# Edge counts in one round: 16 buckets, one product for each block of edges, and a fifth of the row one-hots on ScalarE

## The chip, the cores and the metric

The kernel runs on one core of a Trainium2 chip. The metric is the device time of one execution in microseconds. The engines are TensorE (PE; its weight loads are shown as PEld), VectorE (DVE), ScalarE (ACT), GpSimd (POOL) and SyncE (SP), which issues most DMAs. Each works through its own instructions in order and waits for the others on semaphores.

## What is computed

A model of two layers over 1024 nodes with 512 features and 17408 directed edges (8192 random ones, their reverses, and a loop at each node; sorted by destination in the input). Layer 0: graph attention, then 8 experts of which each row takes two. Layer 1: a graph aggregation with a two-layer network, attention of 8 heads, then 8 experts of which each row takes one. The attention of layer 0 needs the adjacency matrix, the aggregation of layer 1 a matrix with the number of times each edge occurs:

```python
x = x + gnn0(layernorm(x), edge_index)     # adj[src, dst] = 1;  a = q @ k.T / sqrt(512)
                                           # softmax(a * adj + (1 - adj) * -1e6) @ v
x = x + experts0(layernorm(x))
x = x + gnn1(layernorm(x), src, dst)       # neigh = segment_sum(feat[src], dst); relu network; + feat
x = attention_and_experts1(x)              # 8 heads, 8 experts
```

The kernel makes one matrix CT of counts, CT[src, dst] (1024 x 1024). The mask of the attention is min(CT, 1), and CT goes to memory for layer 1. How CT is made is what the change touches.

## The kernel before, in words

**The stages at the front.** The first 307 of 1085 us are: the normalisation of x and its transposes; eight projections (query and key alternating, four each, "projected(i)" on VectorE) of 24 products of 512 columns, since every fp32 product is done in three passes of high and low halves; eight tiles of values; eight tiles of scores (two banks of 512 columns each); the counts; then the attention loop over eight tiles of 128 rows (mask, exponential, transposes, values, residual). For each projection ScalarE makes the high half from PSUM with the bias, VectorE the low half and the low half of a weight block that comes in its place.

**The edges, step 1: sort.** The edges lie on 128 partitions, 136 to each (EC). VectorE tells each edge its tile of 128 sources (in_tile, 8 x 136 wide), counts with a scan (seen_in), and two small products on TensorE give the ranks over the partitions. From them follows for each edge a place: a block of 128 lanes and a lane. Every tile starts a new block, so there are EDGE_BLOCKS = 136 + 8 = 144 blocks.

**Step 2: move.** 136 columns of edges are moved in 34 quads (QUADS). For a quad VectorE makes four pairs of lane one-hots times the edge's row and column number ("lanes", L1085), ScalarE four step functions over the blocks ("steps", L680), and TensorE multiplies them into bank 7: eight edge products of 145 columns ("move_edges", L1623). Two buffers each: quad q waits until quad q-2 has been multiplied. The order is written out by hand. On VectorE one call of lanes() follows projected(0) and the edge columns; then each of projected(1) to projected(7) is followed by two; each low half of a value tile by two; the rest come at the end. On TensorE a move stands after every second quarter (k = 1 and k = 3) of projections 2 to 7, of the value tiles and of the first score tiles. A wait of TensorE at a move holds all that is queued behind it.

**Step 3: count.** From bank 7 follow for each block the rows and columns of its 128 edges (block_rc). VectorE makes 144 row one-hots (count_rows, L1118, 128x128), computes the source tile of each block (tile_past, block_tile), adds the value bias to x (L1126), and makes column one-hots of half the columns, 128x512 (L1138), in groups of four blocks; of every eighth block ScalarE makes the column one-hot with two operations (absolute distance, then relu(1 - d), L713 and L720). A ring of eight groups lies between them and TensorE, which multiplies row and column one-hot of each block into the PSUM bank of its tile (L1697; the bank number comes from a register). Eight banks hold 8 tiles x 512 columns, so there are two rounds over all 144 blocks, one for each half of the columns. After each round ScalarE and VectorE copy the banks to CT (L647, L1143). Then SyncE sends CT out and the attention begins with no_edge (L742), mask (L1153, L1157) and softmax (L749).

## Time and profile before

| | |
|---|---|
| median of 3 runs | 1089.34 us (1089.09 to 1094.71) |
| profiled execution | 1087.22 us, its span 1085.4 us |
| busy in the span | PE 881.8, DVE 757.5, ACT 507.2, POOL 357.7 us |
| instructions | 13783 |

The span runs from the first to the last instruction of the profiled execution; the 1.8 us between it and the execution's own time lie around it. Busy shares of the whole span say little here, since the stages have different limits; the stretches of the first 307 us are what matter for this change. In the rows below, L and a number is a line of the kernel; an idle time stands in square brackets with the operation that ended it.

### The profile page before, as it was taken

What the parts mean: (1) busy time and instruction counts of PE and PEld (TensorE: products, weight loads), DVE (VectorE), ACT (ScalarE), POOL (GpSimd) and SP (SyncE); (2) the same over time, 40 slices, a digit from 0 to 9 for tenths busy, and PEclk for the clock granted to TensorE, in tenths of its full rate; (3) what the DMA queues carried; (4) which work ended last, traced back from release to release, by engine and by line L of the source; (5) the groups of instructions that cost most, each with busy time, mean ns of one, the idle gap of its engine ahead of it and who ended that gap; (6) DMA issues with size and microseconds to landing.
All of it is one profiled execution on the core that took longest, in us unless ns stands there. A gap on an engine that the chain in (4) does not pass through costs nothing.

```text
span 1085.4 us, 13783 instructions
## 1 busy us (share of the span) xinstructions
PE 881.8 (81%) x4522; PEld 674.3 (62%) x4522; DVE 757.5 (70%) x1550; ACT 507.2 (47%) x880; POOL 357.7 (33%) x236
## 2 busy tenths in 40 slices
PE   2999997888864999298898788999999987745990
PEld 2777773336743887077687676777777766534860
DVE  8878599886796443857122776778687877796638
ACT  3567517655652554132303046656565656643530
POOL 1000000000202553007321327686786666703520
PEclk9999999998995999589999889999999999966995
DMA  5010000007261444423111330010010050272432
GB/s 160 30 22 2 1 1 1 1 21 265 66 231 59 137 154 139 164 98 98 49 49 29 107 78 1 20 49 20 11 30 20 1 175 1 87 251 100 154 141 103
DMA packets 55523, 84.74 MB, mean 78 GB/s; under 512 B 8976, under 2 KB 31760, under 8 KB 54944
## 3 DMA queue, kind: packets, MB, share of 16 engines
q1 hardware_dynamic: 49376, 63.94, 18.7%
q0 software_dynamic: 6080, 19.93, 5.6%
q8 instruction: 39, 0.64, 0.2%
q14 instruction: 28, 0.23, 0.1%
HBM read 57.11 MB, written 22.54 MB: 73 GB/s over the span
## 4 chain that ended last, share of the span: by engine, by line
PE 57%; DVE 32%; ACT 4%; issue 3%; DMA 2%; POOL 1%; SPq 0%; DVEq 0%; ACTq 0%; POOLq 0%
PE PS L328 37%; DVE late_columns L1138 4%; DVE neg_max L1507 3%; PE PS L1934 3%; PE PS L1949 3%; DVE APL L976 3%; PE PS L1948 2%; PE PS L1923 2%; DVE count_rows L1118 2%; PE PS L1842 2%; PE PS L1623 2%; PE PS L1785 2%; DVE early_columns L1138 1%; DVE XN L1009 1%; DVE XN L1575 1%
## 5 line engine op out<-in xcount | busy, mean ns | idle before, releaser
L615 POOL TENSOR_SCALAR AP__201<-AP__201,rden 128x1024 f32<-128x1024 f32 x64 | 181.9, 2847 | 84.6 <-DVE rden L1512 83.9
L556 POOL TENSOR_TENSOR W1L<-W1R,W1H 128x1024 fp32r<-128x1024 f32 x8 | 18.9, 2390 | 292.0 <-DVE neg_max L1157 288.2
L647 ACT ACTIVATE APH<-PS 128x512 fp32r<-128x512 f32 x128 | 71.7, 597 | 68.7 <-PE PS L1934 44.1
L1507 DVE TENSOR_REDUCE neg_max<-PS 128x1 f32<-128x1024 f32 x64 | 78.2, 1222 | 34.8 <-PE PS L1923 34.0
L976 DVE TENSOR_TENSOR APL<-PS,APH 128x512 fp32r<-128x512 f32 x128 | 83.1, 680 | 24.8 <-ACT APH L647 24.6
L328 PE MATMUL PS<-XTH,WH 128*128 128x512 f32 x224 | 81.8, 412 | 4.5 <-DVE XTL L976 4.5
L1934 PE MATMUL PS<-ident,AP__201 128*128 128x128 f32 x512 | 70.7, 280 | 12.6 <-DVE APL L976 10.8
L328 PE MATMUL PS<-XTL,WH 128*128 128x512 f32 x224 | 78.4, 397 | 0.0
L328 PE MATMUL PS<-XTH,WL 128*128 128x512 f32 x224 | 78.1, 395 | 0.0
L1934 PEld LDWEIGHTS PS<-ident,AP__201 128*128 128x128 f32 x512 | 59.4, 143 | 28.8 <-issue 16.8
L547 POOL CAST WH<-RAW 128x512 fp32r<-128x512 f32 x30 | 23.4, 781 | 158.5 <-PE PS L328 93.5
L917 ACT ACTIVATE AP__201<-PS,neg_max 128x1024 f32<-128x1024 f32 x64 | 71.5, 1117 | 7.4 <-DVE neg_max L1507 6.7
L566 POOL DMA_INDIRECT BX<-normalised,gather_i x38 | 40.1, 1055 | 90.1 <-DVE scatter_i L1329 69.8
L1085 DVE SCALAR_TENSOR_TENSOR edge_lanes<-lanes,edge_lane,edge_vals 128x256 f16<-128x256 f16 x136 | 55.6, 480 | 8.2 <-PE PS L1623 8.2
L1949 PE MATMUL PS<-APH,AV 128*128 128x512 f32 x128 | 50.8, 397 | 11.1 <-DVE APL L976 11.1
L579 POOL DMA_INDIRECT expert_rows<-BY,scatter_i x38 | 37.4, 985 | 61.9 <-ACT BY L647 61.9
L1602 PE MATMUL PS<-ident,XN 128*128 128x128 f32 x128 | 28.3, 398 | 36.2 <-DVE XN L1009 15.7
L680 ACT ACTIVATE edge_steps<-blocks,edge_step 128x145 f16<-128x145 f16 x136 | 45.3, 408 | 20.7 <-PE PS L1623 17.1
L976 DVE TENSOR_TENSOR BHL<-PS,BHH 128x256 fp32r<-128x256 f32 x38 | 16.1, 425 | 51.2 <-ACT BHH L647 51.2
L1138 DVE TENSOR_SCALAR late_columns<-columns,block_rc 128x512 f16<-128x512 f16 x189 | 50.5, 355 | 0.0
L328 PEld LDWEIGHTS PS<-XTH,WH 128*128 128x128 f32 x224 | 42.2, 193 | 13.4 <-POOL WL L549 3.5
L1697 PE MATMUL PS<-late_columns,count_rows 128*128 128x512 f16 x189 | 46.8, 389 | 4.5 <-DVE late_columns L1138 2.5
(302 smaller groups left out, 2393.4 us busy)
## 6 DMA issues: line engine op xcount, KB each, us to landing
YT<-expert_rows SPq DMA_DIRECT2D x12, 512.0 KB, 6.8
counts<-CT SPq DMA_DIRECT2D x8, 512.0 KB, 4.9
W1R<-in_L_ffn_w SPq DMA_DIRECT2D x8, 512.0 KB, 3.9
W2R<-in_L_ffn_w SPq DMA_DIRECT2D x8, 512.0 KB, 5.6
normalised<-XN SPq DMA_DIRECT2D x2, 2048.0 KB, 8.7
CG<-counts SPq DMA_DIRECT2D x8, 512.0 KB, 3.4
RAW<-in_L_gnn_W SPq DMA_DIRECT2D x16, 256.0 KB, 2.8
W1R<-in_L_ffn_W SPq DMA_DIRECT2D x8, 512.0 KB, 8.7
```

The lines of the kernel that those rows point to most:

```text
L328: got = pe.matmul(o, lhs, r, start=first and j == 0, stop=last and j == 2)
L615: gp.tensor_scalar(AP_[:, i % 4, :], AP_[:, i % 4, :], rden[:, i % 4:i % 4 + 1], None, ALU.mult).then_inc(B["norm"], 1)
L647: act.activation(dst, src, Copy, **kw).then_inc(s, 1)
L680: got = act.activation(edge_steps[:, q % 2, j, 0:STEPS_OF], blocks16[:, :], ACT.Sign, bias=edge_step[:, 4 * q + j:4 * q + j + 1])
L917: act.activation(AP_[:, i % 4, :], banks(2 * (i % 2)), ACT.Exp, bias=neg_max[:, i % 4:i % 4 + 1], accum_out=denom[:, i % 4:i % 4 + 1]).the ...
L976: v.tensor_tensor(dst, src, f(hi), ALU.subtract).then_inc(s, 1)
L1085: got = v.scalar_tensor_tensor(out=edge_lanes[:, q % 2, j, :, :], in0=lanes1[:, :].unsqueeze(1).to_broadcast([P, 2, P]), scalar=edge_lane[ ...
L1138: got = v.tensor_scalar(count_columns(k, j), columns16[:, r * HALF:(r + 1) * HALF], block_rc[:, 1, b:b + 1], None, ALU.is_equal)
L1507: v.tensor_reduce(out=neg_max[:, i % 4:i % 4 + 1], in_=banks(2 * (i % 2)), axis=X_AXIS, op=ALU.max, negate=True).then_inc(B["mx"], 1)
L1697: got = pe.matmul(PS[:, ds(held[b % 24]), :].rearrange("p a n -> p (a n)"), count_rows[:, b, :], moving, start=False, stop=False, skip_gro ...
L1934: got = pe.transpose(PS[:, 4 + half, k * P:(k + 1) * P], AP_[:, i % 4, c * P:(c + 1) * P], ident[:, :])
L1949: got = pe.matmul(PS[:, 6, :], AV[:, hp % 2, h, k, :], APH[:, k, :], start=k == 0, stop=k == NT - 1)
```

## The change

Edges are sorted into 16 buckets: tile of 128 sources times half of the columns. A block then belongs to one half only, so that one product with a column one-hot of 512 columns does for each block, in one round over 136 + 16 = 152 blocks. The arrays of the sort are 16 x 136 wide instead of 8 x 136. Sixteen buckets share eight PSUM banks: bucket k lies in bank k % 8, and ScalarE copies a finished bucket to CT and, for the first eight, writes zeros into the bank. A bucket is finished when its last group has been multiplied; SyncE reads the number of that group from a table into a register and waits for it. Before each pair of groups TensorE waits for a grant from GpSimd, which reads from a table how many banks must be free. The number of the bucket of each block comes from a product on TensorE (past16). All column one-hots are made by VectorE; of the rows every fifth is made by ScalarE from the third score tile on, six behind each copy of the scores. The ring has six groups. The pieces of the sort are spread among projected(0) to projected(3), the first call of lanes() stands behind projected(3), two follow each of projected(4) to projected(7), and TensorE moves its first quad in projection 4; in the score tiles a move stands after every quarter. The value bias is added tile by tile in the attention loop, and ScalarE executes one small exponential before the last bucket. In the diff the names before16, ones16, lanes1, ident are constants; runs of removed lines and of unchanged ones are cut.

```diff
     BLOCKS = tuple((k * N + NEXP * (P - 1)) // P for k in CHOICES)
     QUADS = EC // 4
-    EDGE_BLOCKS = EC + NT
+    BUCKETS = 2 * NT
+    EDGE_BLOCKS = EC + BUCKETS
     COUNT_GROUPS = EDGE_BLOCKS // 4
     STEPS_OF = EDGE_BLOCKS + 1
-    RING = 8
...
+    RING = 6
+    SORTS = (7, 18, 29)
+    PLACED = SORTS[2] + 6
+    assert EC % 4 == 0 and COUNT_GROUPS % 2 == 0 and HB == 2 and GB == 8 and NT == 8 and KT == 4
...
                                  y_d[c * N + 2 * g * P:c * N + (2 * g + 2) * P, :].rearrange("(t p) d -> p t d", p=P)).then_inc(M["y_in"][g], 16)
-        wait(columns_used, 2 * COUNT_GROUPS)
+        wait(sort_dve, PLACED)
+        for k in range(BUCKETS - 1):
+            last = sp.value_load(last_group[0:1, k:k + 1], min_val=1, max_val=COUNT_GROUPS)
+            wait(columns_used, last)
...
                     out=y_d[:, :], out_offset=bass.IndirectOffsetOnAxis(ap=scatter_i[:, b:b + 1], axis=0),
                     in_=BY[:, g % 2, :], in_offset=None).then_inc(M["rows_out"][g % 2], 16)
+        wait(sort_dve, PLACED)
+        for g in range(COUNT_GROUPS // 2):
+            needed = gp.value_load(banks_needed[0:1, g:g + 1], min_val=1, max_val=BUCKETS)
+            wait(bank_free, needed)
+            gp.sem_inc(banks_granted, 1)
         wait(A["m2"], NT)
         expert_lo(0)
...
             act.activation(dst[:, n, :], banks(2 * (i % 2)), Identity, bias=bias[:, n:n + 1]).then_inc(Q0["hi"], 1)
             act.wait_ge(raw_in[j], 16 * (i // 4) + 32)
             copy(WH[:, i, :], RAW[:, j, :], w_hi)
-            if i:
+            if i >= 4:
                 steps()
-            steps()
+            if i >= 3:
+                steps()
         for t in range(NT):
...
             steps()
+        def row_by_act(i):
+            act.wait_ge(distanced, i + 1)
+            act.activation(count_rows[:, 5 * i + 4, :], distance[:, i % 2, :], ACT.Relu, bias=1.0, scale=-1.0).then_inc(act_rows, 1)
         for t in range(NT):
+            for _ in range(min(4, QUADS - stepped[0])):
+                steps()
             act.wait_ge(Q0["s_ps"], t + 1)
             copy(SR[:, t, :], banks((4, 0)[t % 2]), Q0["s_done"], scale=-D ** -0.5)
-            for _ in range(min(2, QUADS - stepped[0])):
...
+            if t == 2:
+                act.wait_ge(sort_dve, PLACED + 3)
+            if 2 <= t < NT - 1:
+                for i in range(6 * (t - 2), 6 * (t - 1)):
+                    if i >= 2:
+                        act.wait_ge(act_rows, i - 1)
+                    act.activation(distance[:, i % 2, :], lanes1[:, :], ACT.Abs, bias=minus_row[:, i:i + 1]).then_inc(distanced, 1)
+                    if i > 6 * (t - 2):
+                        row_by_act(i - 1)
+                row_by_act(6 * (t - 1) - 1)
         assert stepped[0] == QUADS
-        per_round = COUNT_GROUPS // 2
...
+        def count_out(k):
+            if k < BUCKETS - 1:
+                act.wait_ge(bucket_done, k + 1)
+            else:
+                act.wait_ge(columns_used, COUNT_GROUPS)
+            copy(CT[:, k // 2, k % 2 * HALF:(k % 2 + 1) * HALF], PS[:, k % 8, :], counted)
+            if k < 8:
+                act.wait_ge(counted, k + 1)
+                copy(PS[:, k, :], PS[:, k, :], bank_free, scale=0.0)
         def no_edge(half, par):
             t = 2 * half + par
-            act.wait_ge((counted_act, counted_dve)[par], NT // 2 + half + 1)
+            act.wait_ge(counted, 2 * t + 2)
             if t >= 2:
                 act.wait_ge(A["m2"], t - 1)
             act.activation(PEN[:, par, :], CT[:, t, :], ACT.Relu, bias=neg_col[:, 0:1], scale=-NEG).then_inc(A["penalty"], 1)
...
             act.wait_ge(M["w_in"][e // 4], which * (160, 96)[e // 4] + 64)
             copy(W1H[which][:, e, :, :], W1R[:, e, :, :], M["w_hi"])
-        no_edge(0, 0)
...
+        for k in range(BUCKETS):
+            count_out(k)
+            if k in (1, 3):
+                no_edge(0, k // 2)
+            if k == BUCKETS - 2:
...
         v.wait_ge(edges_in, 32)
         v.wait_ge(setup, 12)
-        per_tile = [P, NT, EC]
+        per_bucket = [P, BUCKETS, EC]
         sort(v.tensor_scalar(tile_of[:, :], src_i[:, :], 7, None, ALU.logical_shift_right))
+        sort(v.tensor_scalar(place_i[:, :], dst_i[:, :], 9, None, ALU.logical_shift_right))
         sort(v.tensor_copy(tile_f[:, :], tile_of[:, :]))
-        sort(v.tensor_tensor(in_tile[:, :, :], tile_f[:, :].unsqueeze(1).to_broadcast(per_tile),
...
+        sort(v.scalar_tensor_tensor(out=place_f[:, :], in0=tile_f[:, :], scalar=2.0, in1=place_i[:, :], op0=ALU.mult, op1=ALU.add))
+        sort(v.tensor_tensor(in_bucket[:, :, :], place_f[:, :].unsqueeze(1).to_broadcast(per_bucket),
+                             blocks16[:, 0:BUCKETS].unsqueeze(2).to_broadcast(per_bucket), ALU.is_equal))
         for t in range(NT):
...
             lo(WL[:, u, :], RAW[:, u, :], WH[:, u, :], w_ready)
         transposed(0)
-        v.wait_ge(sort_ps, 1)
...
+        in_flat = in_bucket[:, :, :].rearrange("p t c -> p (t c)")
+        sort(v.tensor_tensor_scan(seen_in[:, 1:1 + BUCKETS * EC], in_flat, in_flat, 0.0, ALU.add, ALU.max))
+        seen_before = seen_in[:, 0:BUCKETS * EC].rearrange("p (t c) -> p t c", t=BUCKETS)
+        seen = seen_in[:, 1:1 + BUCKETS * EC].rearrange("p (t c) -> p t c", t=BUCKETS)
+        sort(v.tensor_tensor(bucket_count16[:, :], seen[:, :, EC - 1], seen_before[:, :, 0], ALU.subtract))
+        assert sorts[0] == SORTS[0]
+        def bucket_bases():
+            v.wait_ge(sort_ps, 1)
+            rank, total = PS[:, 6, 0:BUCKETS], PS[:, 6, BUCKETS:2 * BUCKETS]
+            sort(v.tensor_scalar(bucket_i[:, :], total, P - 1.0, None, ALU.add))
+            sort(v.tensor_scalar(bucket_i[:, :], bucket_i[:, :], 7, None, ALU.logical_shift_right))
+            sort(v.tensor_scalar(bucket_blocks[:, :], bucket_i[:, :], 1.0, None, ALU.max))
+            sort(v.tensor_tensor_scan(bucket_end[:, :], ones16[:, 0:BUCKETS], bucket_blocks[:, :], 0.0, ALU.mult, ALU.add))
+            sort(v.tensor_tensor(bucket_base[:, :], bucket_end[:, :], bucket_blocks[:, :], ALU.subtract))
+            sort(v.scalar_tensor_tensor(out=bucket_base[:, :], in0=bucket_base[:, :], scalar=float(P), in1=rank, op0=ALU.mult, op1=ALU.add))
+            sort(v.tensor_tensor(bucket_base[:, :], bucket_base[:, :], seen_before[:, :, 0], ALU.subtract))
+            sort(v.tensor_tensor(seen, seen, bucket_base[:, :].unsqueeze(2).to_broadcast(per_bucket), ALU.add))
+            sort(v.tensor_tensor(end_mask[0:BUCKETS, :], bucket_end[0:BUCKETS, :], ident[0:BUCKETS, 0:BUCKETS], ALU.mult))
+            sort(v.tensor_reduce(out=end_col[0:BUCKETS, :], in_=end_mask[0:BUCKETS, :], axis=X_AXIS, op=ALU.add))
+            sort(v.tensor_scalar(past16[0:BUCKETS, :], blocks16[0:BUCKETS, 0:EDGE_BLOCKS], end_col[0:BUCKETS, :], None, ALU.is_ge))
+            assert sorts[0] == SORTS[1], sorts
+        def places():
+            sort(v.tensor_tensor(in_bucket[:, :, :], in_bucket[:, :, :], seen, ALU.mult))
+            sort(v.tensor_reduce(out=place_f[:, :], in_=in_bucket[:, :, :].rearrange("p t c -> p c t"), axis=X_AXIS, op=ALU.add))
+        def edge_columns():
+            sort(v.tensor_scalar(place_i[:, :], place_f[:, :], -1.0, None, ALU.add))
+            sort(v.tensor_scalar(place_i[:, :], place_i[:, :], 7, None, ALU.logical_shift_right))
+            sort(v.tensor_copy(edge_block[:, :], place_i[:, :]))
+            sort(v.scalar_tensor_tensor(out=edge_lane[:, :], in0=edge_block[:, :], scalar=-float(P), in1=place_f[:, :], op0=ALU.mult, op1=ALU.add))
+            sort(v.tensor_scalar(edge_vals[:, :, 0], src_i[:, :], 1.0, 0.5, ALU.add, ALU.mult))
+            sort(v.scalar_tensor_tensor(out=edge_vals[:, :, 0], in0=tile_f[:, :], scalar=-0.5 * P, in1=edge_vals[:, :, 0], op0=ALU.mult, op1=ALU.add))
+            sort(v.tensor_scalar(dst_i[:, :], dst_i[:, :], HALF - 1, None, ALU.bitwise_and))
+            sort(v.tensor_scalar(edge_vals[:, :, 1], dst_i[:, :], 0.5, None, ALU.mult))
+            sort(v.tensor_scalar(edge_step[:, :], edge_block[:, :], -1.0, -0.5, ALU.mult, ALU.add))
+            assert sorts[0] == SORTS[2], sorts
+        def banks_of_blocks():
+            v.wait_ge(sort_ps, 2)
+            sort(v.tensor_scalar(block_f[:, :], PS[:, 6, 2 * BUCKETS:2 * BUCKETS + EDGE_BLOCKS], BUCKETS - 1.0, None, ALU.min))
+            sort(v.tensor_copy(block_bank[:, :], block_f[:, :]))
+            sort(v.tensor_scalar(block_bank[:, :], block_bank[:, :], 7, None, ALU.bitwise_and))
+            sort(v.tensor_scalar(banks_needed[:, :], block_f[:, :].rearrange("p (g j) -> p g j", j=8)[:, :, 7], 1.0, None, ALU.add))
+            sort(v.tensor_scalar(last_group[:, :], bucket_end[:, :], 3.0, None, ALU.add))
+            sort(v.tensor_scalar(last_group[:, :], last_group[:, :], 2, None, ALU.logical_shift_right))
+            assert sorts[0] == PLACED, sorts
         def projected(i):
...
             got.then_inc(edges_laned, 1)
         projected(0)
-        sort(v.tensor_scalar(place_i[:, :], place_f[:, :], -1.0, None, ALU.add))
...
+        bucket_bases()
+        projected(1)
+        places()
+        projected(2)
+        edge_columns()
+        projected(3)
         lanes()
-        for i in range(1, 2 * KT):
+        for i in range(4, 2 * KT):
             projected(i)
+            if i == 5:
+                banks_of_blocks()
             lanes()
             lanes()
         for t in range(NT):
...
         v.wait_ge(edges_moved, QUADS)
         sort(v.tensor_copy(block_sum[:, :, :], PS[:, 7, 0:2 * STEPS_OF].rearrange("p (v b) -> p v b", v=2)))
         sort(v.tensor_tensor(block_rc[:, :, :], block_sum[:, :, 1:STEPS_OF], block_sum[:, :, 0:EDGE_BLOCKS], ALU.subtract))
-        sort(v.tensor_scalar(minus_column[:, :], block_rc[:, 1, :], -1.0, None, ALU.mult))
+        sort(v.tensor_scalar(minus_row[:, :], block_rc[:, 0, 0:EDGE_BLOCKS - 2].rearrange("p (i j) -> p i j", j=5)[:, :, 4], -1.0, None, ALU.mult))
         v.wait_ge(Q0["v_ps"], NT)
         for b in range(EDGE_BLOCKS):
+            if b % 5 == 4:
+                continue
             got = v.tensor_scalar(count_rows[:, b, :], lanes1[:, :], block_rc[:, 0, b:b + 1], None, ALU.is_equal)
         got.then_inc(rows_ready, 1)
-        per_block = [P, EDGE_BLOCKS, NT]
...
+        for k in range(COUNT_GROUPS):
+            if k >= RING:
+                v.wait_ge(columns_used, k - RING + 1)
+            elif k == 2:
+                v.wait_ge(Q0["s_ps"], NT)
+            for j in range(4):
+                b = 4 * k + j
+                got = v.tensor_scalar(count_columns(k, j), columns16[:, 0:HALF], block_rc[:, 1, b:b + 1], None, ALU.is_equal)
+            got.then_inc(columns_ready, 1)
         v.wait_ge(row0_in, 16)
-        v.tensor_tensor(X[:, :, :], X[:, :, :], row0[:, :].unsqueeze(1).to_broadcast([P, NT, D]), ALU.add).then_inc(Q0["bias"], 1)
...
+        def value_bias(t):
+            v.tensor_tensor(X[:, t, :], X[:, t, :], row0[:, :], ALU.add).then_inc(Q0["bias"], 1)
         def mask(half, par):
             t = 2 * half + par
-            v.wait_ge((counted_act, counted_dve)[par], NT // 2 + half + 1)
+            v.wait_ge(counted, 2 * t + 2)
             v.wait_ge(Q0["s_done"], NT)
             if t >= 2:
                 v.wait_ge(A["exp"], t - 1)
...
         mask(0, 0)
         mask(0, 1)
+        value_bias(0)
         p_lo(0, 0)
         for i in range(NT // 2 - 1):
             mask(i + 1, 0)
+            value_bias(2 * i + 1)
             p_lo(i, 1)
             residual(i, 0)
             mask(i + 1, 1)
+            value_bias(2 * i + 2)
             p_lo(i + 1, 0)
             residual(i, 1)
+        value_bias(NT - 1)
         p_lo(NT // 2 - 1, 1)
         v.wait_ge(gw_hi, 1)
...
             return [PS[:, b, :], PS[:, b + 1, :]]
         pe.wait_ge(setup, 12)
-        pe.wait_ge(sort_dve, SORTS[0])
...
         moved = [0]
...
                                  k == 0, k == KT - 1)
                 if k == KT - 1:
                     got.then_inc(Q0["ps"], 1)
-                if i >= 2 and k % 2:
+                if i >= 4 and k % 2:
                     move_edges()
+            if i == 0:
+                pe.wait_ge(sort_dve, SORTS[0])
+                pe.matmul(PS[:, 6, 0:BUCKETS], before16[:, :], bucket_count16[:, :], start=True, stop=True)
+                pe.matmul(PS[:, 6, BUCKETS:2 * BUCKETS], ones16[:, :], bucket_count16[:, :], start=True, stop=True).then_inc(sort_ps, 1)
+            elif i == 3:
+                pe.wait_ge(sort_dve, SORTS[1])
+                pe.matmul(PS[:, 6, 2 * BUCKETS:2 * BUCKETS + EDGE_BLOCKS], ones16[0:BUCKETS, :], past16[0:BUCKETS, :],
+                          start=True, stop=True).then_inc(sort_ps, 1)
         pe.wait_ge(w_ready, 12)
         for par in range(2):
...
                                  k == 0, k == KT - 1)
                 if k == KT - 1:
                     got.then_inc(Q0["s_ps"], 1)
-                if k % 2 and moved[0] < QUADS:
+                if moved[0] < QUADS:
                     move_edges()
         tiles = [pe.alloc_register(f"tile{j}") for j in range(24)]
         pe.wait_ge(rows_ready, 1)
-        pe.wait_ge(sort_dve, SORTS[1] + 6)
+        pe.wait_ge(act_rows, EDGE_BLOCKS // 5)
+        pe.wait_ge(sort_dve, PLACED)
         pe.wait_ge(Q0["v_done"], NT)
-        for r in range(2):
...
+        pe.wait_ge(Q0["s_done"], NT)
+        for t in range(8):
+            pe.matmul(PS[:, t, :], count_rows[:, EDGE_BLOCKS - 1, :], columns16[:, 0:HALF], start=True, stop=True).then_inc(bank_free, 1)
+        for g in range(COUNT_GROUPS):
+            if g % 6 == 0:
+                n = min(24, EDGE_BLOCKS - 4 * g)
+                pe.load(tiles[0:n], block_bank[0:1, 4 * g:4 * g + n])
+                held = [pe.snap(q, min_val=0, max_val=7) for q in tiles[0:n]]
+            if g % 2 == 0:
+                pe.wait_ge(banks_granted, g // 2 + 1)
+            pe.wait_ge(columns_ready, g + 1)
+            for j in range(4):
+                b = 4 * g + j
+                got = pe.matmul(PS[:, ds(held[b % 24]), :].rearrange("p a n -> p (a n)"), count_rows[:, b, :],
+                                count_columns(g, j), start=False, stop=False, skip_group_check=True)
+            got.then_inc(columns_used, 1)
         for q in tiles:
             pe.free_register(q)
```

## Rows read from the trace of the kernel before

**Rows 1.** The table of stretches: busy time of each engine, then granted clock, DMA share, GB/s.
```profile
27.70:81.50 53.80, 51.21 (x289) 40.81 (x289) 43.50 (x87) 30.80 (x72) 0.00 (x0) 1.00 0.13 26
81.50:114.50 33.00, 33.00 (x225) 25.47 (x226) 30.04 (x71) 24.23 (x68) 0.00 (x0) 0.95 0.01 1
114.50:134.70 20.20, 20.20 (x123) 16.02 (x122) 9.13 (x23) 9.18 (x24) 0.00 (x0) 1.00 0.00 1
134.70:162.00 27.30, 27.23 (x120) 22.15 (x119) 27.16 (x149) 4.62 (x6) 0.00 (x0) 1.00 0.00 1
162.00:248.20 86.20, 69.67 (x304) 29.97 (x305) 80.27 (x268) 57.36 (x86) 0.00 (x0) 0.96 0.07 26
```

**Rows 2.** The chain of waits, 134 to 260 us: start, duration, what.
```profile
135.93 23.53 DVE count_rows L1118 x144
...
162.42 4.44 DVE X L1126
166.88 1.93 DVE early_columns L1138 x7
168.81 5.51 DVE late_columns L1138 x21
...
241.38 2.06 ACT CT L647 x4
...
245.53 1.28 ACT L749
246.82 1.25 ACT PR L749 x2
248.21 1.95 PE PS L1710 x8
...
259.92 1.24 DVE SM L1153
```

**Rows 3.** The chain of waits, 60 to 100 us.
```profile
78.40 1.12 ACT KH L688
79.55 1.28 DVE KL L979
...
81.49 2.93 PE PS L328 x6
84.41 0.75 PE PS L1623 x8
...
90.52 0.53 PE PS L1623 x8
91.05 1.44 PE PS L328 x6
```

**Rows 4.** VectorE in order of time: start, duration, operation, idle before it.
```profile
87.87 3.25 DVE L1085 SCALAR_TENSOR_TENSOR edge_lanes<-lanes,edge_lane,edge_vals 128x256 f16<-128x256 f16 x8
91.19 0.69 DVE L976 TENSOR_TENSOR VL<-PS,VH 128x512 fp32r<-128x512 f32 x1
```

**Rows 5.** ScalarE in order of time, values and scores.
```profile
86.63 0.60 ACT L647 ACTIVATE VH<-PS 128x512 fp32r<-128x512 f32 x1
...
161.96 1.02 ACT L647 ACTIVATE SR<-PS 128x1024 f32<-128x1024 f32 x1 [4.41 <-PE PS L328]
```

**Rows 6.** VectorE in order of time, the sort of the edges.
```profile
5.67 2.43 DVE L1036 TENSOR_TENSOR_SCAN seen_in<-in_tile 128x1088 f32<-128x1088 f32 x1
...
28.98 1.29 DVE L1062 TENSOR_TENSOR seen_in<-seen_in,tile_base 128x1088 f32<-128x1088 f32 x1
...
31.64 2.25 DVE L1064 TENSOR_REDUCE place_f<-in_tile 128x136 f32<-128x1088 f32 x1
```

**Rows 7.** TensorE in order of time, behind two idle stretches.
```profile
81.49 0.79 PE L328 MATMUL PS<-WH,XTH 128*128 128x512 f32 x1 [2.59 <-DVE WL L976]
...
207.91 3.16 PE L1697 MATMUL PS<-late_columns,count_rows 128*128 128x512 f16 x7 [2.02 <-DVE late_columns L1138]
```

**Rows 8.** VectorE in order of time, in the attention loop.
```profile
264.63 1.23 DVE L976 TENSOR_TENSOR PTL<-PS,PTH 128x1024 fp32r<-128x1024 f32 x1 [2.15 <-ACT PTH L647]
```

More of the change, by code:

```diff
@@ L429, in _ @@
         results(0)
-        wait(Q0["bias"], 1)
+        wait(Q0["bias"], NT)
         sp.dma_start(row0[:, :], a["L1_gnn_b2"].partition_broadcast(P)).then_inc(row0_in, 16)
@@ L722, in counts_out @@
-        def counts_out(r):
-            act.wait_ge(columns_used, COUNT_GROUPS * (r + 1))
-            for t in range(0, NT, 2):
-                copy(CT[:, t, r * HALF:(r + 1) * HALF], PS[:, t, :], counted_act)
-        act.wait_ge(sort_dve, SORTS[1] + 3)
-        column_distance(0)
-        for i in range(2 * per_round):
-            if i + 1 < 2 * per_round:
-                column_distance(i + 1)
-            column(i)
-            if i == per_round + 1:
-                counts_out(0)
-        counts_out(1)
+            if t == 2:
+                act.wait_ge(sort_dve, PLACED + 3)
@@ L1051, in _ @@
         transposed(0)
-        v.wait_ge(sort_ps, 1)
-        tile_rank, tile_total = PS[:, 6, 0:NT], PS[:, 6, NT:2 * NT]
-        sort(v.tensor_scalar(tile_i[:, :], tile_total, P - 1.0, None, ALU.add))
-        sort(v.tensor_scalar(tile_i[:, :], tile_i[:, :], 7, None, ALU.logical_shift_right))
-        sort(v.tensor_copy(tile_blocks[:, :], tile_i[:, :]))
-        sort(v.tensor_tensor_scan(tile_end[:, :], ones16[:, 0:NT], tile_blocks[:, :], 0.0, ALU.mult, ALU.add))
-        sort(v.tensor_tensor(tile_base[:, :], tile_end[:, :], tile_blocks[:, :], ALU.subtract))
@@ L1060, in _ @@
-        sort(v.scalar_tensor_tensor(out=tile_base[:, :], in0=tile_base[:, :], scalar=float(P), in1=tile_rank, op0=ALU.mult, op1=ALU.add))
-        sort(v.tensor_tensor(tile_base[:, :], tile_base[:, :], seen_before[:, :, 0], ALU.subtract))
-        sort(v.tensor_tensor(seen, seen, tile_base[:, :].unsqueeze(2).to_broadcast(per_tile), ALU.add))
-        sort(v.tensor_tensor(in_tile[:, :, :], in_tile[:, :, :], seen, ALU.mult))
-        sort(v.tensor_reduce(out=place_f[:, :], in_=in_tile[:, :, :].rearrange("p t c -> p c t"), axis=X_AXIS, op=ALU.add))
+        in_flat = in_bucket[:, :, :].rearrange("p t c -> p (t c)")
@@ L1119, in _ @@
         got.then_inc(rows_ready, 1)
-        per_block = [P, EDGE_BLOCKS, NT]
-        sort(v.tensor_tensor(tile_past[:, :, :], tile_end[:, :].unsqueeze(1).to_broadcast(per_block),
-                             blocks16[:, 0:EDGE_BLOCKS].unsqueeze(2).to_broadcast(per_block), ALU.is_le))
-        sort(v.tensor_reduce(out=block_f[:, :], in_=tile_past[:, :, :], axis=X_AXIS, op=ALU.add))
-        sort(v.tensor_scalar(block_tile[:, :], block_f[:, :], NT - 1.0, None, ALU.min))
-        v.wait_ge(row0_in, 16)
@@ L1172, in residual @@
             v.wait_ge(A["rden"], t + 1)
+            v.wait_ge(Q0["bias"], t + 1)
             x = X[:, ds(t), :].rearrange("p a n -> p (a n)")
@@ L1673, in _ @@
         pe.wait_ge(rows_ready, 1)
-        pe.wait_ge(sort_dve, SORTS[1] + 6)
+        pe.wait_ge(act_rows, EDGE_BLOCKS // 5)
+        pe.wait_ge(sort_dve, PLACED)
         pe.wait_ge(Q0["v_done"], NT)
-        for r in range(2):
-            for t in range(NT):
-                if r:
-                    pe.wait_ge((counted_act, counted_dve)[t % 2], t // 2 + 1)
-                elif t == 0:
-                    pe.wait_ge(Q0["s_done"], NT)
-                pe.matmul(PS[:, t, :], count_rows[:, EDGE_BLOCKS - 1, :], columns16[:, 0:HALF], start=True, stop=True)
-            for g in range(COUNT_GROUPS):
-                if g % 6 == 0:
-                    pe.load(tiles, block_tile[0:1, 4 * g:4 * g + 24])
-                    held = [pe.snap(q, min_val=0, max_val=NT - 1) for q in tiles]
-                pe.wait_ge(columns_ready, COUNT_GROUPS * r + g + 1)
-                for j in range(4):
-                    b = 4 * g + j
-                    k = COUNT_GROUPS * r + g
-                    moving = count_columns(k, j)
-                    if b % 8 == 7:
-                        pe.wait_ge(act_columned, k // 2 + 1)
-                        moving = act_columns[:, k // 2 % 4, :]
-                    got = pe.matmul(PS[:, ds(held[b % 24]), :].rearrange("p a n -> p (a n)"), count_rows[:, b, :],
-                                    moving, start=False, stop=False,
-                                    skip_group_check=True)
-                got.then_inc(columns_used, 1)
@@ L1721, in values @@
             got.then_inc(A["av_ps"], 1)
-        pe.wait_ge(counted_act, NT)
-        pe.wait_ge(counted_dve, NT)
+        pe.wait_ge(counted, BUCKETS)
         p_transposes(0, 0)
```

91 lines of the change are left out of this document (25 added, 66 removed).

## The prediction

> **What bounds the kernel now.** I read the stretches of the two stages first, then the chain of waits through them, then single instructions of VectorE and ScalarE. From 27.7 to 162.0 us TensorE is busy 131.6 of 134.3 us: projections, values and scores of the first attention fill it, and the 34 quads of edge products lie between them [rows 1]. VectorE is nearly full beside it (30.0 of 33.0 us while the values are made). After 162.0 the roles change: TensorE is busy 69.7 of 86.2 us, VectorE 80.3 [rows 1]. The chain there is VectorE's one-hots: 144 rows of counts in 23.5 us from 135.9, the 4.4 us addition of the value bias, then columns without a break, 21 in 5.51 us, 0.263 each [rows 2]. It makes 126 in each of two rounds. When the last product is done, at 241.4, come copies and penalties to 245.5, a table load of 1.3 us and an exponential of 1.25 before the first probability tile is transposed at 248.2 [rows 2]. Nothing behind that tile depends on the change, save the bias.
>
> So two sums are needed: when the scores end (last copy of scores begins at 161.96 [rows 5]), and how long from there to the first transpose (248.21 − 161.96 = 86.3 us).
>
> **Part 1: after the scores, 43.8 us less.** Both rounds become one: 152 columns where 252 were made by VectorE. Rows and the first 8 columns fit under the scores as before: from the edges' end, 1.2 us of differences, 122 rows at 0.163 = 19.9, 8 columns 2.1, together 23, while TensorE has 30 us of scores left (22 quarter tiles at 5.44/4, the period of a tile being 4.41 + 1.03 [rows 5]). The shorter row list itself thus gives nothing: scores cover it, and the value bias and the table of tiles, 5 us beyond the scores' end today (166.88 against 161.96), leave the path. From the scores' end remain 144 columns × 0.263 = 37.8 us; about 0.7 for the ring of six, as TensorE starts only 3 to 4 us later (copy of scores, eight clearing products); two steps of the first mask at 1.24, 2.5 us behind the last column (they run under the final copies today); the exponential and its hand-off 1.35 [rows 2]. Sum 42.35; with a little for more hand-offs 42.5. The table load is done ahead and the copies go bucket by bucket beside the products. TensorE needs 0.96 us at most for four products (six take 1.44 [rows 3]) against VectorE's 1.05, so it isn't the bound. ScalarE copies out and clears in two half copies of 0.60, as the values' high half [rows 5], for 2.5 us of columns in a bucket. The grants of banks and the marks of finished buckets pass through register loads on GpSimd and SyncE that no row shows; I take nothing, as a pair of groups leaves them 2.1 us and eight banks lie between use and reuse. The other end is 3 us a pair, 19 × 0.9 = 17 us. ScalarE's 30 rows are two operations each, six rows in each of five tiles: at 0.60, the copy four times as wide, 7.2 us of a tile's 5.4, which would add up to 9 us; I take 0.35 for 128 elements, 4.2 us, hidden. The value bias, now eight additions of some 0.6 us, falls into VectorE's waits of 2.15 us before each low half [rows 8]; uncovered it would be 4.9 us. 86.3 − 42.5 = 43.8 us gained.
>
> **Part 2: before the scores end, what the new order of the edges costs.** I counted for each move of a quad (8 edge products) which instruction on VectorE makes its lanes. Today VectorE has laned 2i − 1 quads when it comes to "projected(i)", and TensorE, in the last quarter of projection i, wants quad 2i − 2: one in hand. In the new order there are 2i − 7 in hand (first quad after projected(3)), and TensorE (first move in i = 4) wants 2i − 6: one short. That quad is made behind projected(i), which itself waits for projection i's last product. TensorE's queue stands at the move, with the whole next projection behind it. The same holds for the values: 9 + 2t laned before tile t's low half, and its second move wants 10 + 2t. ScalarE's steps are short in the same way but come earlier. Today's margin is seen in the rows: TensorE runs through the values without a gap [rows 1], and VectorE's quads and low halves follow each other in a period of 3.32 + 0.6 = 3.92 us [rows 4].
>
> Each stall is a chain of known pieces. In a projection: ScalarE's biased copy 1.12, the low half 1.28, and the weights' low half with the hand-offs for the rest of the 3.09 us from 78.40 to 81.49 [rows 3], then one quad 1.66 [rows 4]: 4.8 us, four times, 19.2. At i = 5 six small operations for the banks come between, 1.4. At i = 7 the present wait of TensorE for the value weights (2.59 us of idle [rows 7]) is swallowed, −2.6. Together 18.0. In a value tile: high half 0.60 [rows 5], low half 0.69 and a quad 1.66 (two in the 3.32 us from 87.87 to 91.19 [rows 4]), hand-offs 0.1: 3.05 us, eight times, 24.4.
>
> The start of this: the arrays of the sort are twice as long. The scan (2.43 at 1088 elements [rows 6]) takes about 4.7, now after the last transposed tile; the addition 1.29 becomes 2.45, the product likewise, the reduction 2.25 becomes 4.45 [rows 6]. VectorE: scan and count to 31.8; projected(0) to 35.9; bases 4.5, to 40.5; projected(1) 42.4; places 6.9, 49.4; projected(2) 51.3; nine edge columns 53.8; projected(3) 55.7; first quad 57.4. TensorE comes to projection 4 at 50 and waits 1.0 us for the low half, reaches the first move at 53.4 and waits 4.0. Together 5.0.
>
> Small terms: normalisation starts earlier, since the scan leaves its front, −0.7; three small products +0.5; edge products of 153 columns for 145, 34 × 0.53 × 8/145 = +1.0 [rows 3]. Moves end in tile 2 of the scores as before, and there VectorE (1.66) keeps up with 1.36 + 0.56 us.
>
> Without the clock: 5.0 + 18.0 + 24.4 + 0.8 = 48.2 us.
>
> **The clock.** After the 2.59 us of idle before 81.49 six products take 2.93 us, not 1.44, and the eight edge products 0.75, not 0.53: the 1.2 GHz level for about 3.4 us, 1.7 us lost [rows 3, 7]. After the idle of 2.02 before 207.91 seven products take 3.16 us, where 7 × 0.24 = 1.7 would be the full rate, again the lower level [rows 7]. The new order has 13 idle stretches of 3 to 6 us. If every one costs 1.7 it is 22 us; if none does, 0, and the 1.7 paid today comes back. Some of a slow stretch passes while TensorE still idles, and a slow stretch doesn't follow every gap at once, so I take 0.6: 13.3 − 1.7 = 11.6 us. The scores end 59.8 us later.
>
> The Trainium skill ("TensorE: Matmul & The Clock Gate", HAM oscillation — how this bites in real kernels) says that a loop with waits between bursts of matmuls starts every burst at half clock and pays each time. By it the loss is the full 22, and the sum 8.7 us more. Both gaps above agree with it; thirteen in a row no row here shows.
>
> **Sum.** 59.8 − 43.8 = +16.0. The profiled execution took 1087.2 us (span 1085.4 and 1.8 around it), so 1103.2; the median of the runs is 2.1 higher, by that 1105.3. I say 1104.
>
> **Rivals.** (a) *TensorE isn't held by the short quads* (the change does what it says: half the columns). For it: 43.8 us lie on VectorE's chain and are really gone. Against it: engines work in order and the count of quads is one short in every step. It needs only the start 5.0 and 0.8: 1087.2 + 5.8 − 43.8 = 1049. The turning point is the mean cost of one of the twelve later stalls, clock included: (43.8 − 5.8)/12 = 3.2 us. Above it the change loses, below it wins; I have (18.0 + 24.4 + 11.6)/12 = 4.5. (b) *The stalls come, the clock holds*: 48.2 − 1.7 − 43.8 = +2.7, 1090 to 1092. For it: two gaps are all that I have, and the value tiles' 3.05 us lie between bursts of full work. Against: 2.02 and 2.59 us were enough. (c) *The clock falls at every gap*: 48.2 + 22 − 1.7 − 43.8 = +24.7, 1112 to 1114. (d) *Register loads on GpSimd or SyncE pace the counting*, 3 us for a pair of groups: +16 + 17, 1120 to 1122. For it: each grant and mark passes an engine that has no part in the counting today.
>
> **Chances.** Forecast with its neighbour (c): 0.72; (b) 0.10; (a) 0.11; (d) 0.07. The range takes in (b) and (c): 1090 to 1115. Within 0.5% (5.4 us) is what a measurement can't tell from no change: faster by more 0.11, within 0.11, slower by more 0.78.
>
> **What would show it.** TensorE idle in front of the edge products (the second move of each projection from 4 on and of each value tile), some 4.8 and 3.05 us each, released by VectorE's lanes; in the value tiles a period of 7 to 8.7 us, not 3.92, and a granted clock of 0.75 to 0.9; the last score copy near 222, not 162; from there to the first transpose about 42.5 us; 152 column one-hots with hardly a wait; no added idle in the attention loop. I'd be wrong if TensorE ran through the values without gaps, or if the counting took over 50 us.

## The result and the profile after

The changed kernel takes 1117.64 us (median of four, 1115.39 to 1120.88) where the kernel before takes 1090.2 (four, 1089.09 to 1094.71): ratio 1.0254, 95% interval 1.0212 to 1.0296. The forecast, 1104 with a range of 1090 to 1115, had the sign and the place of the loss right, and the part of the clock much too small. The profiled execution has a span of 1117.6 us, 32.2 more than before.

The table of stretches of the profile after has the columns of [rows 1]. The second and third stretch are the projections from the first move on and the value tiles; the fourth is the scores, the fifth goes from their end to the first transpose of the attention.

```profile
27.60:59.30 31.70, 27.12 (x111) 21.47 (x112) 26.80 (x36) 7.90 (x12) 0.00 (x0) 0.99 0.11 28
59.30:118.30 59.00, 38.55 (x168) 29.89 (x168) 21.51 (x46) 16.59 (x41) 0.00 (x0) 0.77 0.06 9
118.30:190.00 71.70, 47.83 (x233) 36.46 (x234) 34.12 (x81) 27.46 (x81) 0.00 (x0) 0.76 0.00 1
190.00:235.90 45.90, 45.84 (x244) 36.73 (x243) 34.90 (x162) 33.43 (x96) 0.00 (x0) 1.00 0.00 1
235.90:278.00 42.10, 35.72 (x160) 15.54 (x160) 41.38 (x148) 19.78 (x30) 0.00 (x0) 1.00 0.03 10
```

Where TensorE ran through [rows 1] it now idles 20.5 of 59.0 and 23.9 of 71.7 us, and the granted clock, 0.95 to 1.00 before, is 0.77 and 0.76. The list of waits of TensorE, up to 350 us (total, times, longest), names the place:

```profile
PE PS L1666 <- DVE edge_lanes L1136: 47.8, 13, 6.2
...
PE PS L335 <- DVE QL L996: 1.1, 1, 1.1
...
PE PS L1741 <- DVE early_columns L1180: 0.9, 1, 0.9
PE PS L1741 <- POOLq L520: 0.8, 1, 0.8
PE PS L1741 <- DVE late_columns L1180: 0.7, 2, 0.3
```

Thirteen waits before the edge products (L1666) for the lanes of VectorE, where the kernel before had none worth a row. The chain of waits shows two of them whole, one in projection 5, one in the first value tile (start, duration, what):

```profile
77.33 1.12 ACT KH L706
78.47 1.28 DVE KL L996
79.76 0.60 DVE WL L993
81.79 1.69 DVE edge_lanes L1136 x4
83.52 1.21 PE PS L1666 x8
84.73 5.02 PE PS L335 x12
...
118.25 0.60 ACT VH L665
118.88 0.69 DVE VL L993
119.57 1.59 DVE edge_lanes L1136 x4
121.21 1.21 PE PS L1666 x8
122.42 2.65 PE PS L335 x6
125.06 1.05 PE PS L1666 x8
```

TensorE's last product of projection 5 ends at 77.3, its next edge products begin at 83.52: copy, low half, weights, the six small operations (80.4 to 81.8), the quad. There the eight edge products take 1.21 us, not 0.56, and the twelve products behind them 5.02 us, not 2.82: the 1.2 GHz level, and not for 3.4 us as in [rows 3] but for about 5.6 us (an estimate: 1.21, and 4.4 of the 5.02, since twelve products wholly at half rate would take 5.64). The edge products come at 121.21, 130.99, 139.40, 148.12, 156.51, 165.22, 175.17 and 183.67 in the eight value tiles, a period of 8.9 us against 3.92 [rows 4].

Behind the scores all is as it was summed. First the chain of waits, then the engines in order of time at the first transpose:

```profile
235.87 1.03 ACT SR L665
237.04 1.69 PE PS L1730 x7
239.78 1.05 PE PS L1741 x4
240.85 2.19 DVE early_columns L1180 x8
243.04 4.20 DVE late_columns L1180 x16
...
272.45 2.10 DVE early_columns L1180 x8
274.55 1.14 DVE SM L1194
```

```profile
278.37 1.07 PE L1753 MATMUL PS<-ident,PR 128*128 128x128 f32 x8 [2.09 <-ACT PR L762]
...
279.28 0.69 DVE L1185 TENSOR_TENSOR X<-X,row 128x512 f32<-128x512 f32 x1
```

From the last score copy (235.87) to the first transpose (278.37) it is 42.5 us, where it was 86.3 [rows 2, 5]. One grant of GpSimd was waited for, 0.8 us.

### The profile page after: what moved, and what is told of

It reads as the page before. It is cut to its first block, busy times and chain, and to the rows that moved or that the text cites. A ratio compares the mean times of both kernels' runs of the same rounds, so it can differ in the third digit from the quotient of the medians.

```text
span 1117.6 us, 13358 instructions
## 1 busy us (share of the span) xinstructions
PE 878.6 (79%) x4379; PEld 680.3 (61%) x4379; DVE 731.3 (65%) x1436; ACT 486.0 (43%) x885; POOL 358.1 (32%) x236
## 4 chain that ended last, share of the span: by engine, by line
PE 57%; DVE 32%; ACT 4%; issue 4%; DMA 1%; POOL 1%; DVEq 0%; SPq 0%; POOLq 0%; ACTq 0%
PE PS L335 37%; PE PS L1976 3%; PE PS L1991 3%; DVE neg_max L1553 3%; PE PS L1666 3%; PE PS L1965 3%; DVE APL L993 2%; PE PS L1990 2%; PE PS L1884 2%; DVE late_columns L1180 2%; DVE edge_lanes L1136 2%; PE PS L1827 2%; DVE XN L1026 1%; DVE stats L1001 1%; DVE early_columns L1180 1%
## 5 line engine op out<-in xcount | busy, mean ns | idle before, releaser
L665 ACT ACTIVATE APH<-PS 128x512 fp32r<-128x512 f32 x128 | 71.7, 597 | 70.1 <-PE PS L1976 45.7
L1976 PE MATMUL PS<-ident,AP__204 128*128 128x128 f32 x512 | 71.2, 281 | 11.6 <-DVE APL L993 10.8
L1666 PE MATMUL PS<-edge_steps,edge_lanes 128*128 128x153 f16 x272 | 32.3, 278 | 47.8 <-DVE edge_lanes L1136 47.8
L1666 PEld LDWEIGHTS PS<-edge_steps,edge_lanes 128*128 128x128 f16 x272 | 23.9, 119 | 60.6 <-DVE edge_lanes L1136 53.6
L1648 PEld LDWEIGHTS PS<-ident,XN 128*128 128x128 f32 x128 | 23.9, 213 | 49.4 <-issue 24.2
L335 PEld LDWEIGHTS PS<-XTL,WH 128*128 128x128 f32 x224 | 44.3, 198 | 9.2
```

Of the source, the lines that this page charges most:

```text
L335: got = pe.matmul(o, lhs, r, start=first and j == 0, stop=last and j == 2)
L665: act.activation(dst, src, Copy, **kw).then_inc(s, 1)
L1648: got = pe.transpose(PS[:, t % 4, k * P:(k + 1) * P], src[:, t, k * P:(k + 1) * P], ident[:, :])
L1666: got = pe.matmul(PS[:, 7, n * STEPS_OF:(n + 1) * STEPS_OF], edge_lanes[:, q % 2, j, n, :], edge_steps[:, q % 2, j, 0:STEPS_OF], start=c = ...
L1976: got = pe.transpose(PS[:, 4 + half, k * P:(k + 1) * P], AP_[:, i % 4, c * P:(c + 1) * P], ident[:, :])
```

## The experiments

They ran in three sets, with the kernel before beside them in each (1088.9, 1089.0 and 1088.0 us). Times are medians, ratios those to the kernel before with their 95% interval. The first set is again, skip1, fill and one_ahead, the second b_short, rows_dve, fill6 and warm, the third fill2 and fillv.

**again.** The changed kernel, unchanged.

> The changed kernel once more, beside the others. Both theories: about 1117 us, ratio 1.02 to 1.03, as the granted clock of each run falls a little otherwise. It is the measure for the runs beside it.

1113.89 us, ratio 1.0236 (1.0215 to 1.0258). The last score copy begins at 228.2 us here, at 235.9 in the first profile, with the same 47.7 us of waits. TensorE is busy 152.2 us between the first projection and that copy, and was busy 159.3 us in the first profile, for the same products; 0.5 us is an earlier start. Of the 7.1 us of busy time 1.8 lie in projection 0, ahead of all the waits: in the first profile its first eight products take 3.6 us, here 1.9, though the clock row shows 1.00 for them there (fill's are as slow at the same place, with a clock row of 0.50). Projections 4 to 7 are alike in the two (38.55 and 38.60 us). The rest, 5.5 us, lies in the value tiles, where two of the eight gaps are followed by full rate here (chain of waits, the first of them):

```profile
119.02 0.71 PE PS L1666 x8
119.73 1.43 PE PS L335 x6
```

**one_ahead.** The old margin in the new kernel.

```diff
-                if i >= 4 and k % 2:
+                if i >= 5 and k % 2:
                     move_edges()
...
             projected(i)
-            if i == 5:
-                banks_of_blocks()
-            lanes()
-            lanes()
+            for _ in range((1, 3, 2, 2)[i - 4]):
+                lanes()
...
-            if i >= 4:
-                steps()
-            if i >= 3:
+            for _ in range((0, 0, 0, 1, 1, 3, 2, 2)[i]):
                 steps()
...
         while laned[0] < QUADS:
             lanes()
+        banks_of_blocks()
```

> The changed kernel with the old margin: moves start in projection 5; one quad of lanes and steps behind projections 3 and 4, three behind 5, two behind 6 and 7; the six small operations for the banks behind the last quad. My theory: no wait of TensorE over 1 us from projection 4 to the scores' end, clock 1.00, the scores end at 165 to 168 us, from there 42.5 us to the first transpose as in the changed kernel; 1087.2 + 4 - 43.9 = 1047 us (1044 to 1052). Rival (order doesn't matter): near 1117. If only part of the waits goes: 1060 to 1090.

1049.81 us, ratio 0.9638 (0.9621 to 0.9656): it is faster than both kernels. Its waits of TensorE and its stretches:

```profile
PE PS L335 <- DVE WL L991: 2.6, 1, 2.6
PE PS L335 <- DVE XTL L991: 1.4, 1, 1.4
PE PS L1663 <- DVE edge_lanes L1134: 1.4, 1, 1.4
```

```profile
27.00:80.00 53.00, 50.17 (x243) 39.90 (x243) 42.11 (x67) 21.24 (x43) 0.00 (x0) 1.00 0.13 27
80.00:165.00 85.00, 82.60 (x504) 65.28 (x505) 75.47 (x257) 64.76 (x181) 0.00 (x0) 0.98 0.00 1
165.00:210.00 45.00, 38.16 (x173) 17.30 (x172) 42.08 (x149) 21.22 (x36) 0.00 (x0) 1.00 0.04 15
```

One wait of 1.4 us instead of thirteen of 47.8 (a little over the 1.0 that was expected), the clock near 1.00, the last score copy at 167.1, the first transpose at 209.7: 42.6 us apart again. The order of the quads is the loss, and the single round is worth what was summed. (The six small operations also moved, behind the last quad; that was 1.4 us of the forecast's sum.)

**skip1.** Only TensorE's side of it.

```diff
-                if i >= 4 and k % 2:
+                if 4 * i + k > 17 and k % 2:
                     move_edges()
```

> The changed kernel, but TensorE starts its moves one place later (in the last quarter of projection 4, not in its second), so that every later move wants a quad that is one earlier. My theory (quads one short): the 4.8 us waits before the edge products of projections 4 to 7 vanish; in the value tiles the wanted quad is the second one behind the previous low half, ready 0.60 + 0.69 + 3.3 = 4.6 us after the tile before against a period of 4.0, so about 0.6 us of wait is left in each, without a fall of the clock. The scores end near 172 us instead of 236, the whole takes 1050 to 1058 us. Rival (the longer arrays of the sort and the wider edge products slow this stretch, the order doesn't matter): within 5 us of the changed kernel.

1067.25 us, ratio 0.9796 (0.9776 to 0.9817): faster than before, as the theory has it against its rival, but 9 us past the expected range. My count was wrong. The chain of waits shows which move stalls:

```profile
92.68 1.45 PE PS L335 x6
94.12 0.02 issue
94.14 0.61 ACT VH L665
94.75 0.02 issue
94.77 0.69 DVE VL L993
95.47 1.59 DVE edge_lanes L1136 x4
97.06 0.04 issue
97.10 0.71 PE PS L1666 x8
97.82 1.45 PE PS L335 x6
```

It is the first move of each value tile, not the second: it wants the first quad behind the previous low half, 3.0 us after that tile, and TensorE is there after 0.56 + 1.44 = 2.0. So TensorE waits 1.0 us in each of eight tiles, in a period of 5.14 us, and the clock stays up through the tiles. The projections aren't free of waits either, as had been expected: four waits make up the rest of 13.5 us in twelve. The longest, 2.9 us before 72.73 in projection 5, is followed by eight edge products in 1.21 us and twelve products in 5.11, so the clock fell there and cost about 2.8 us. With 13.5 us of waits where 8 × 0.6 = 4.8 were expected that is 11.5 us more than I had, against a time 9 to 17 us above the expected 1058 to 1050.

**b_short.** The reverse: the kernel before, its moves put too early.

```diff
-                if i >= 2 and k % 2:
+                if i >= 1 and k % 2:
                     move_edges()
```

> The kernel before with one condition changed: TensorE's moves start in projection 1, not in 2, so that each wants a quad two later than now (VectorE and ScalarE unchanged). Nothing of the buckets is in it. My theory (the place of the moves against the quads is the whole loss): 4.3 us before the first move, 4.8 us in each of projections 1 to 7 less the 2.6 us wait of today, 3.05 in each value tile: 59.7 us of waits, and about 2.0 us of clock for each of 16 gaps as the changed kernel showed, less 1.7: 30 us. The counting starts earlier under the scores, -7. Sum +83: 1172 us (1160 to 1182). Rival (the waits belong to the 16 buckets, their longer sort and their 153 columns): within 10 us of the kernel before.

1176.41 us, ratio 1.0797 (1.0766 to 1.0828). The waits of TensorE:

```profile
PE PS L1623 <- DVE edge_lanes L1085: 61.3, 16, 4.7
PE PS L1623 <- ACT edge_steps L680: 4.9, 2, 2.4
```

With no bucket in it, this kernel loses 87 us by one digit (each move wants a quad two later than before; 1172 was expected). So neither the longer sort nor the 153 columns are needed for the stalls.

**fill.** The stalls stay, TensorE works through them.

```diff
+        def keep_busy(n):
+            for _ in range(n):
+                pe.matmul(PS[:, 5, :], XTH[:, 0, 0:P], XTH[:, 0, 0:HALF], start=True, stop=True)
...
                 if i >= 4 and k % 2:
+                    if k == 3 or i == 4:
+                        keep_busy(19 if k == 3 else 15)
                     move_edges()
...
+                if k == KT - 1:
+                    keep_busy(12)
                 if k % 2:
                     move_edges()
```

> The changed kernel with idle products into an unused bank before each stalled move (15 before the first, 19 in each projection from 4 on, 12 in each value tile, 0.227 us each); the moves come no earlier. My theory (waits of 48 us and, apart from them, 26 us more loss by the clock than before): TensorE stays at full clock, the waits stay in length but are filled, 1117 - 24 = about 1093 us (1089 to 1097). Rival (products are slower there for another reason, or the idle time is the whole loss): no gain, 1115 us or more.

1094.4 us, ratio 1.0048 (1.0030 to 1.0066). The stretches:

```profile
60.00:110.00 50.00, 46.59 (x247) 36.88 (x246) 24.01 (x52) 19.67 (x49) 0.00 (x0) 1.00 0.04 2
110.00:167.00 57.00, 55.16 (x333) 42.95 (x332) 33.70 (x81) 26.31 (x77) 0.00 (x0) 1.00 0.00 1
```

The clock is 1.00 in both. The last score copy begins at 210.4 us, 48.4 after that of the kernel before; the sum "without the clock" was 48.2. To compare them, 1.8 has to be taken off the 48.4 for slow products in projection 0 (clock 0.50 from 26.4 to 30.1 us), and the 1.7 added that the kernel before loses by the clock and fill doesn't: 48.3. Filling the waits gives back 1113.9 − 1094.4 = 19.5 us: the clock's part of the loss in this set of rounds.

**fillv**: as fill, with only the value tiles filled (the three lines in the projections left out).

> As fill, but only the waits in the value tiles are filled, those of the projections (4.0, 4.8, 6.2, 4.8, 4.8 us) are not. Theory: the five long gaps carry 2 to 2.5 us of clock each, 10 to 12 us: 1105 us (1102 to 1109); then the eight value tiles carry the other half of the 20 to 26 us. Rival: nearly all of the loss is in the value tiles: 1094 to 1098.

1103.56 us, ratio 1.0130 (1.0105 to 1.0155): 9.2 us over fill, so the five long gaps in the projections (3.4 to 6.2 us) cost 1.8 us each, and the eight of 3.0 us the other 10.3, 1.3 each. The three kernels ran in two sets, and each ratio is known to about 2.5 us, so the two prices are good to about 0.7 and 0.5 us a gap. The rival, that nearly all of the loss is in the value tiles, falls.

**fill6 and fill2**: as fill, with 6 and with 2 products instead of 12 in a value tile (the argument of the second keep_busy).

> The kernel with idle products before the stalled moves (fill), with 6 instead of 12 in each value tile, so that about 1.6 us of each 3.05 us wait stay idle. Theory A (a gap has its price only where it is long; 2.02 us was the shortest seen to cost): the clock stays up, 1094 us as fill. Theory B (what counts is the share of idle time in a stretch of such tiles, 1.6 of 7.0 us, or every wait costs): 8 tiles at 1 to 2 us more, 1102 to 1110 us.

> As fill, with 2 idle products instead of 12 before the stalled move of each value tile: 2.6 us of each wait stay idle (6 products, 1.65 us idle, cost nothing). Theory A (a gap costs from somewhere between 1.65 and 2.59 us on): the clock falls behind most of the eight, 1 to 2 us each: 1100 to 1110 us. Theory B (a gap of this size costs only with a gap before it, or after longer rest): 1094 to 1097.

fill6: 1094.57 us, ratio 1.0048 (1.0035 to 1.0061), the same as fill. TensorE waits 16.1 us for lanes here instead of 5.3, with gaps of 1.6 us in the value tiles, and pays nothing; the tiles:

```profile
110.00:167.00 57.00, 45.65 (x292) 34.89 (x291) 33.64 (x80) 27.46 (x80) 0.00 (x0) 1.00 0.00 1
```

fill2: 1098.96 us, ratio 1.0108 (1.0082 to 1.0133), 4.6 us over fill, between its two theories: gaps of 2.5 us cost 0.6 us on the mean of eight. The trace shows which: behind the first four TensorE is busy 4.6 us until the next gap, the full rate, behind the next three 5.9 to 6.2, so four cost nothing and from the fifth on each costs 1.3 to 1.6 us. What makes the difference stays open.

**rows_dve**: one_ahead with all rows on VectorE.

```diff
-            if b % 5 == 4:
-                continue
             got = v.tensor_scalar(count_rows[:, b, :], lanes1[:, :], block_rc[:, 0, b:b + 1], None, ALU.is_equal)
```

(and without ScalarE's row operations and TensorE's wait for them)

> The kernel with the old margin (one_ahead), but all 152 rows made by VectorE and none by ScalarE. My theory: rows lie under the scores; 1.2 + 152 x 0.163 + 2.1 = 28 us on VectorE against 27.3 us of scores left, so 0 to 1.5 us slower than one_ahead: 1050 to 1052 us. Rival (the fifth of the rows on ScalarE carries part of the gain, 30 x 0.163 = 4.9 us): 1055.

1051.09 us, ratio 0.9639 (0.9611 to 0.9666), against 0.9638 of one_ahead: no difference that can be told. The row one-hots on ScalarE bring nothing that shows; the scores cover the rows either way.

**warm**: one_ahead with products in two pauses.

```diff
+        keep_busy(10, 5)
         pe.wait_ge(w_ready, 12)
...
         pe.wait_ge(counted, BUCKETS)
+        keep_busy_sr(5, 0)
         p_transposes(0, 0)
```

> one_ahead with 10 idle products in the 2.6 us wait before the first value tile and 5 in the wait before the first transpose of the attention. Theory: each gap is followed by a slow stretch, 1.7 us behind the first, 2.2 behind the second; filled, both go: 1050 - 4 = 1046 us. Rival: the waits are not what makes the clock fall there, or the filling delays the products behind it: 1050 or more.

1049.04 us (1044.70 to 1051.47), ratio 0.9618 (0.9580 to 0.9657): inconclusive as a time, the interval holds both no gain and the 4 us. The traces say more: the six products behind the wait for the value weights take 1.66 us, where one_ahead's take 2.92, the eight edge products behind them 0.56 instead of 0.85, and the first 24 value products of the attention 5.75 instead of 6.39. Both slow stretches are gone, 2.2 us in this execution.

## Why the prediction was right and where it was wrong

*The place and length of the stalls*: right. Forecast 1.0 us for the low half and 49 us before the moves (4.0 + 4 × 4.8 + 1.4 + 24.4), found 1.1 and 47.8 (3.4 before the first move, 4.7 in three projections, 6.2 in projection 5, 3.0 in each value tile); fill confirms the whole sum of that part (48.3 against 48.2), b_short and one_ahead that the order of the quads makes it.

*The gain behind the scores*: right, 43.8 forecast, 86.3 − 42.5 = 43.8 found; 42.6 us from scores' end to transpose in one_ahead too. That the shorter row list gives nothing was right as well (rows_dve); ScalarE's two operations for a row took 0.40 and 0.29 us where 0.35 each had been taken without a row. The grants through registers cost 0.8 us once, so rival (d) falls. The addition of the bias stayed in VectorE's waits for the most part: the first residuals of the attention loop follow each other in 7.47 us, as before, but for one step of 7.83, and from the first to the last of eight it is 49.6 us, where it was 48.7.

*Rival (a)* was wrong for this kernel, but close to what one more quad in hand makes of it: 1049 forecast for TensorE not being held, 1049.8 measured in one_ahead. That they agree within 1 us is in part luck: (a) counts 4.0 us before the first move, of which one_ahead keeps 1.4, while one_ahead's profile has a slow start in projection 0 that (a) lacks. Its turning point holds too: skip1, with 13.5 us in twelve waits and one slow stretch, 1.4 us a stall, clock included, instead of 4.5, is on the winning side.

*The clock*: the step that failed. I took 0.6 × 13 × 1.7 = 13.3 us and held 22 for the upper end. The scores end 73.9 us later in the first profile, not 59.8. TensorE idles 208.3 − 159.3 = 49.0 us from 27.6 to 235.9 against 2.7 before, +46.3 (forecast: 47.4, and −0.7 for an earlier start, of which 0.1 came here, where the statistics had to wait for x, and 0.6 in again). It is busy 159.3 against 131.6 us [rows 1], +27.7, of which 1.5 are the wider and the additional products, as forecast, and 26.2 the clock's, where the forecast had 11.6. With the 1.7 of before that is 27.9 in all: 1.8 in projection 0, ahead of every wait, and 26.1 behind the 13 gaps, 2.0 each, against the 1.0 each (0.6 × 1.7) of the forecast. In again the same working gives 152.2 − 131.6 + 1.7 − 1.5 = 20.8, 1.6 each.

Both factors of the term were too small. The 0.6 stood for gaps without a price and for slow time that passes while TensorE idles; in the first profile slow products follow every one of the 13 gaps, in again 11 of them. And the 1.7 was the loss of the one slow stretch of [rows 3], of 3.4 us; the clock rows above give 2 × (0.23 × 59.0 + 0.24 × 71.7) = 61.6 us at the lower level for 13 gaps, 4.7 each, some of them longer, as behind the wait in projection 5 (5.02 + 1.21 against 2.82 + 0.56: 2.85 us lost). The "upper end" was no bound: it took the one slow stretch that was shown for the longest possible, and so the range and rival (c), 1112 to 1114, ended below the 1117.6 measured. In the later rounds filling the gaps gave back 19.5 us and the kernel took 1113.9, inside the range. The two sets differ by 3.7 us in the medians; their profiles differ by 7.6 us at the scores' end, 7.1 of them the clock's. What makes the clock fall behind one gap and not behind another like it stays open.

The Trainium skill ("TensorE: Matmul & The Clock Gate", HAM oscillation — how this bites in real kernels) says of a loop with a long wait behind each short burst that every burst starts at half clock and pays for it. The changed kernel agrees for its gaps of 3 to 6 us in the first profile, and in again for all but two of 3.0 us. The 22 us that I worked out with it, from my own 1.7, was nearer to 26.1 and 20.8 than my 13.3. fill6 shows that waits of 1.6 us in each tile don't have that price, and four of fill2's eight waits of 2.5 us didn't.

*The rest*: 2.1 us. Behind the first transpose the first 24 value products take 7.86 us where they took 5.75:

```profile
282.86 7.86 PE PS L335 x24
290.75 0.76 DVE X L1216
```

Before, TensorE paused 6.9 us there; the granted clock was 0.53 in the last 3.2 us of the pause and 0.50 through the 16 transposes behind it, and the value products ran at full rate. Now it pauses 2.1 us, the first eight transposes run at full rate, and the slow stretch (0.54 from 280.0 to 287.3 us) falls on the others and on ten of the products. I hadn't a term for it. From the first transpose to the first residual it is 2.3 us more, the rest of the loop takes 0.9 more, and all that comes behind 1.1 less; no run took these two last apart. Sum in the profiles: 235.87 − 161.96 = 73.9, −43.8, +2.1 = 32.2 us, the difference of the spans.

## What to carry to other kernels

Where an in-order engine consumes what another makes piece by piece, count for each consumer the number of the piece it wants and the number made before the producer's own next wait for that consumer: one short costs the full round trip each time, one more in hand costs nothing. Price such a stall with the clock: 47.8 us of idle time in gaps of 3 us and more cost 20.8 us on top in one execution and 26.1 in another, and a single slow stretch in a profile is no upper bound. A change that loses can hold a real gain: the same counting, with a few lines of order changed, takes 3.6% off the kernel.

## What the runs showed of the hardware

The mean price of a gap in TensorE's work grew with its length here: nothing for 1.6 us (fill6 against fill, eight gaps), 0.6 us for 2.5 (fill2 against fill), 1.3 for 3.0 (again against fillv), 1.8 for 3.4 to 6.2 (fillv against fill, five gaps). Single gaps lie far from the mean: four of the 2.5 us cost nothing and four 1.3 to 1.6, and two of the eight of 3.0 us in again cost nothing. And 187 products that compute nothing (91 in the projections, 12 in each of eight value tiles) made the kernel 19.5 us faster than leaving TensorE idle in the same waits.
